# Four of nine taps of the interpolation matrices transposed by DMA, sampling two tiles behind

## The chip, the cores and the metric

The kernel runs on one core of one Trainium2 chip. The metric is the device time of one execution, in microseconds (us).

## What is computed

The input is x, four images of 128 channels and 64 x 64 pixels, in float32. Two layers follow each other.

```
# layer 0: attention over the 4096 pixels of each image
h = group_norm(x); q, k, v = split(qkv_w @ h + qkv_b)
x = x + proj_w @ (softmax(q^T k * C**-0.5) v) + proj_b

# layer 1: deformable convolution block
out = relu(batchnorm(conv2d(x, w1), g1, b1))
offsets = conv2d(out, w_off) + b_off          # 18 = 9 taps x (row, column)
out = batchnorm(deform_conv(out, offsets, w2), g2, b2)
return relu(out + x)

# deform_conv: for each pixel and each of 9 taps n
px = row + pn_x + off[..., :9];  py = col + pn_y + off[..., 9:]    # clipped
xo = bilinear interpolation of out at (px, py)
y  = sum over taps and channels of w2[:, :, tap] * xo[tap]
```

## The kernel before

All matrix products that need more than half precision are made of three products of f16 parts: `three` (L937 to L939) multiplies high by high, high by low and low by high, and adds them in PSUM.

The program has three parts: attention (until about 1710 us), the first convolution with the offset convolution (until about 2046 us), and the deformable stage, which the change touches. The deformable stage works on 128 tiles (q) of 128 pixels, 32 to an image; 16 tiles make a half image. A tile has 8 blocks (t) of 4 x 4 pixels. For each block the 120 pixels around it (a window of 10 rows by 12 columns) are in SBUF, one pixel to a partition, and for each of the 9 taps (k) an interpolation matrix of 128 pixels by 120 window positions tells how each output pixel is mixed from its window. These are the steps of a tile:

- SyncE loads the windows of two tiles at a time (`xt_windows`, L290 to L296): three transfers of 40 partitions and 8 KB each, into one of four buffers. The read pattern of a transfer has 10 rows as its outermost dimension, the written tile 40 partitions.
- GpSimd multiplies the row hats by the column hats into `interp` (SS, f32, 128 pixels x 9 taps x 120, two buffers), three instructions (L372). Before tile q it waits until TensorE has transposed tile q-2. Twice per half image it also computes the distances of the next one (L358, L363), which ScalarE turns into hats in four instructions at tiles 10 to 13 (L559, L562).
- TensorE transposes the nine matrices against an identity, three to a PSUM bank (L1105).
- ScalarE casts each bank to f16 (`interpT_hi`, L541), VectorE subtracts that from the bank to get the rest (`interpT_lo`, L876). Both tiles are laid out as block, tap, 16 pixels, in two buffers.
- TensorE samples: for each block a `three` with the window as weights and the 144 columns of the transposed matrices as moving operand (`sample`, L1117), 24 products in three sections. ScalarE and VectorE split the result into `sampled_hi` (L550) and `sampled_lo` (L884).
- TensorE applies the second convolution (`conv2`, L1126, 27 products of 128 columns), VectorE adds the result to `y_then_z` (L892) and takes statistics every fourth tile (L899).

The order on TensorE is written out by hand: in step g it does the transposes of tile q, then in three sections the sampling of tile q-1 and the convolution of tile q-2. The other engines follow the same steps. TensorE and VectorE run the steps in a loop over half images, ScalarE and GpSimd in one over pairs of half images, SyncE in one over images. Semaphores count each step; `after(eng, key, count)` waits for one. If all offsets are small, as with these inputs, the stage is passed through once.

In the attention part the kernel already transposes by DMA: SyncE issues transfers of 128 x 512 f16 (L242, L244), beside transposes on TensorE.

Of the kernel before, what the change touches and what calls it, by code (L numbers as in the profile page):

```python
# [17 lines left out]
F32 = mybir.dt.float32  # L18
# [19 lines left out]
TAPS = 9  # L38
# [21 lines left out]
NBUF = 4  # L60
SECT = ((0, 3), (3, 3), (6, 2))
# [26 lines left out]
def build(nc, x, weights, consts, out):  # L88
# [6 lines left out]
    with ctx:  # L95
# [3 lines left out]
        def sb_in(scope, name, shape, dt):  # L99
# [9 lines left out]
        ZT = sb_in(ctx, "zeros_f16", [128, 768], F16)  # L109
        CNT = sb_in(ctx, "pass_counts", [1, 6], I32)  # L110
        HIGH = sb_in(ctx, "offset_high", [128, GPI, NOFF], F32)
# [36 lines left out]
        XS = sb_in(l1, "xt_stage", [128, 2, 4, 2 * C], F16)  # L148
        l1a = ExitStack()
        XC = sb_in(l1a, "x1_rows", [128, 4, 512], F32)  # L150
# [11 lines left out]
        STh = sb_in(l1b, "interpT_hi", [128, 2, 8, TAPS, 16], F16)  # L162
        STl = sb_in(l1b, "interpT_lo", [128, 2, 8, TAPS, 16], F16)
# [26 lines left out]
        s_ld = [sem(f"windows_loaded{i}") for i in range(NBUF)]  # L190
        s_fx = [sem(f"final_loaded{i}") for i in range(B)]
# [12 lines left out]
            tt="interp_transposed", th="interpT_hi_ready", tl="interpT_lo_ready", mm="sampled",  # L204
# [18 lines left out]
        def _(sp):  # L223
# [36 lines left out]
            sp.wait_ge(s_pz, 1)  # L260
# [16 lines left out]
            for i in range(2):  # L277
                stored(sp, s_xs[i], B * NCH * 2)
            after(sp, "l1", L1_FLAG)
# [5 lines left out]
            with sp.Fori(0, ny) as iy:  # L285
                with sp.Fori(0, nx) as ix:
                    with sp.Fori(0, B) as b:
                        for i in range(HH // TW):

                            after(sp, "mm", (iy * SX + ix) * (3 * GROUPS) + b * (3 * GPI) + 6 * (i - (NBUF - 1)))  # L290
                            row = (iy + sy0) * WR + b * IMG_ROWS + (GUARD + TW * i - 3 - WR * (SY // 2))
                            slot = row * PITCH + (ix + sx0) * (WC // TW) + (0 - (WC // TW) * (SX // 2))
                            for a in range(WC // TW):
                                src = bass.AP(xt_dram.tensor, (slot + a) * (2 * C),
                                              [[PITCH * 2 * C, WR], [SLOTS * 2 * C, TW], [1, WW // TW * 2 * C]])
                                sp.dma_start(XW[WR * TW * a:WR * TW * a + WR * TW, i % NBUF, :, :], src).then_inc(s_ld[i % NBUF], 16)  # L296
# [11 lines left out]
        def _(po):  # L308
            for k in s:
                po.sem_inc(s[k], OPEN)  # L310
            for k in s_xo + s_xs + s_tr:
                po.sem_inc(k, OPEN)
# [921 lines left out]
```

## Time and profile before

| | us |
|---|---|
| median of 3 runs | 2662.31 |
| lowest and highest | 2656.64, 2663.07 |
| profiled execution | 2665.29 |
| its span, first to last instruction | 2663.5 |
| TensorE busy in the span | 2492.9 (94%) |
| VectorE busy | 1925.3 (72%) |
| ScalarE busy | 1823.4 (68%) |
| GpSimd busy | 953.9 (36%) |

The page gives each engine's busy time over the whole span, which mixes the three parts of the program. Its rows in 40 slices show them apart: a slice is 66.6 us, and the deformable stage fills the last nine but the very last. What one tile costs is read in stretches of 4 us inside a half image. Starts of instructions come from the timeline, where an idle time in square brackets stands with what ended it. Matmuls overlap in the pipeline, so the duration of one (220 ns and more) is longer than the distance between two starts.

### The profile page before, as it was taken

Reading aid. Unit: us, or ns where it says so; the run is one execution under the profiler, and the core shown is the slowest. Engines: PE = TensorE matmul, PEld = TensorE weight load, DVE = VectorE, ACT = ScalarE, POOL = GpSimd, SP = SyncE. Lnnn points to the kernel's source line nnn. Section 1 sums busy time; section 2 is a strip of 40 time slices with the busy share of each in tenths; the row PEclk is TensorE's granted clock in tenths of the full one; section 3 lists DMA queues with packets and bytes.
Section 4 is the critical chain, followed back from the end, with each engine's and each line's share of the span. In section 5 each row is a group of like instructions: output and inputs, shape, how many; then the busy total and the mean of one; then the engine's idle time right before and its main releaser. Section 6 shows DMA issues by size and latency. Waiting matters only on the chain.

```text
span 2663.5 us, 75563 instructions
## 1 busy us (share of the span) xinstructions
PE 2492.9 (94%) x27789; PEld 1960.8 (74%) x27789; DVE 1925.3 (72%) x3815; ACT 1823.4 (68%) x2963; POOL 953.9 (36%) x939
## 2 busy tenths in 40 slices
PE   4999999999999999999999999899975999999993
PEld 2777777777777777777777777644443999999993
DVE  6778877788877788887777777522264877877775
ACT  4778777777877777877777777511264766766664
POOL 1333333333333333333333333200012666656650
PEclk9999999999999999999999999899997999999997
DMA  2545554545564545554444444543122444333336
GB/s 78 123 92 96 94 114 91 95 95 94 96 116 86 96 96 92 95 90 84 94 96 95 95 94 95 143 136 132 37 73 79 138 117 121 116 110 116 111 106 253
DMA packets 642462, 278.30 MB, mean 104 GB/s; under 512 B 565665, under 2 KB 625569, under 8 KB 633889
## 3 DMA queue, kind: packets, MB, share of 16 engines
q1 hardware_dynamic: 642208, 274.82, 44.9%
q8 instruction: 171, 2.80, 0.5%
q14 instruction: 83, 0.67, 0.1%
HBM read 98.76 MB, written 41.68 MB: 53 GB/s over the span
## 4 chain that ended last, share of the span: by engine, by line
PE 89%; DVE 3%; DMA 2%; issue 2%; ACT 1%; SPq 1%; POOL 0%; DVEq 0%; POOLq 0%; ACTq 0%
PE psum L937 16%; PE psum L938 16%; PE psum L939 16%; PE psum L976 9%; PE psum L978 8%; PE psum L977 8%; PE psum L962 8%; PE psum L1105 5%; PE psum L1078 1%; DMA xt_scratch<-xt_stage 1%; DMA final<-x_scratch 1%; PE psum L1007 1%; SPq L276 0%; DVE padded_hi L842 0%; DMA probsT_dma_lo<-probs_lo 0%
## 5 line engine op out<-in xcount | busy, mean ns | idle before, releaser
L328 POOL TENSOR_TENSOR probs_lo<-probs,probs_hi 128x512 f16<-128x512 f32 x512 | 593.2, 1159 | 1085.7 <-ACT probs_hi L427 1085.7
L630 DVE TENSOR_REDUCE neg_max<-psum 128x1 f32<-128x1024 f32 x512 | 627.1, 1225 | 320.8 <-PE psum L939 320.4
L424 ACT ACTIVATE probs<-psum,exp_bias 128x1024 f32<-128x1024 f32 x512 | 570.8, 1115 | 193.3 <-DVE exp_bias L632 163.1
L937 PE MATMUL psum<-k_hi,q_hi 128*128 128x512 f16 x1024 | 389.3, 380 | 5.7 <-DVE vT_lo L744 4.0
L938 PE MATMUL psum<-k_lo,q_hi 128*128 128x512 f16 x1024 | 389.6, 380 | 0.0
L939 PE MATMUL psum<-k_hi,q_lo 128*128 128x512 f16 x1024 | 389.5, 380 | 0.0
L976 PE MATMUL psum<-vT_hi,probsT_dma_hi 128*128 128x129 f16 x2048 | 374.5, 221 | 4.3 <-DMA probsT_dma_lo<-probs_lo 4.3
L417 ACT ACTIVATE probsT_hi<-psum 128x512 f16<-128x512 f32 x512 | 303.7, 593 | 103.9 <-PE psum L962 103.9
L978 PE MATMUL psum<-vT_hi,probsT_lo 128*128 128x129 f16 x2048 | 374.3, 219 | 0.0
L976 PE MATMUL psum<-vT_hi,probsT_hi 128*128 128x129 f16 x2048 | 374.2, 221 | 0.0
L977 PE MATMUL psum<-vT_lo,probsT_hi 128*128 128x128 f16 x2048 | 374.1, 218 | 0.0
L978 PE MATMUL psum<-vT_hi,probsT_dma_lo 128*128 128x129 f16 x2048 | 374.1, 219 | 0.0
L977 PE MATMUL psum<-vT_lo,probsT_dma_hi 128*128 128x128 f16 x2048 | 374.0, 218 | 0.0
L372 POOL TENSOR_TENSOR interp<-row_hats,col_hats 128x360 f32<-128x360 f32 x384 | 294.7, 796 | 216.6 <-PE psum L1105 211.7
L640 DVE TENSOR_TENSOR probsT_lo<-psum,probsT_hi 128x512 f16<-128x512 f32 x512 | 350.1, 684 | 2.9 <-ACT probsT_hi L417 2.7
L427 ACT ACTIVATE probs_hi<-probs 128x512 f16<-128x512 f32 x512 | 322.6, 630 | 22.6 <-DMA probsT_dma_lo<-probs_lo 0.6
L962 PEld LDWEIGHTS psum<-constants,probs 128*128 128x128 f32 x2048 | 254.2, 141 | 94.3 <-issue 0.5
L962 PE MATMUL psum<-constants,probs 128*128 128x128 f32 x2048 | 307.9, 273 | 0.0
L876 DVE TENSOR_TENSOR interpT_lo<-psum,interpT_hi 120x384 f16<-120x384 f32 x384 | 191.5, 551 | 84.7 <-ACT interpT_hi L541 83.7
L550 ACT ACTIVATE sampled_hi<-psum 128x432 f16<-128x432 f32 (+1 forms) x384 | 182.6, 496 | 91.7 <-PE psum L939 91.7
L884 DVE TENSOR_TENSOR sampled_lo<-psum,sampled_hi 128x432 f16<-128x432 f32 (+1 forms) x384 | 207.0, 554 | 52.4 <-ACT sampled_hi L550 48.2
L541 ACT ACTIVATE interpT_hi<-psum 120x384 f16<-120x384 f32 x384 | 162.4, 491 | 87.5 <-PE psum L1105 85.2
(158 smaller groups left out, 5754.2 us busy)
## 6 DMA issues: line engine op xcount, KB each, us to landing
xt_windows<-xt_scratch SPq DMA_DIRECT2D x192, 320.0 KB
xt_scratch<-zeros_f SPq DMA_DIRECT2D x28, 576.0 KB, 4.0
x_image<-x SPq DMA_DIRECT2D x4, 2048.0 KB, 8.3
probsT_dma_hi<-probs_hi SPq DMA_TRANSPOSE x512, 2.4
probsT_dma_lo<-probs_lo SPq DMA_TRANSPOSE x512, 2.5
x_residual<-x SPq DMA_DIRECT2D x128, 64.0 KB, 2.1
x_scratch<-x_out SPq DMA_DIRECT2D x128, 64.0 KB, 1.8
x_rows<-x_scratch SPq DMA_DIRECT2D x32, 256.0 KB, 3.0
```

The lines of the kernel that those rows point to most:

```text
L328: po.tensor_tensor(PHl[:, j, :], P[:, j, 0:512], PHh[:, j, :], ALU.subtract).then_inc(s["pl"], 1)
L424: act.activation(P[:, j, :], sc, ACT.Exp, bias=NB[:, par, j:j + 1]).then_inc(s["exp"], 1)
L427: act.activation(PHh[:, j, :], P[:, j, 0:512], ACT.Copy).then_inc(s["ph"], 1)
L630: ve.tensor_reduce(NM[:, par, j:j + 1], sc, AX.X, ALU.max, negate=True).then_inc(s["mx"], 1)
L640: ve.tensor_tensor(PTl[:, k, :, :].rearrange("p m q -> p (m q)"), PS[:, 4 + j % 2, :], PTh[:, k, :, :].rearrange("p m q -> p (m q)"), ALU. ...
L937: pe.matmul(dst, lh, rh, start=start, stop=False)
L938: pe.matmul(dst, lh, rl, start=False, stop=False)
L939: return pe.matmul(dst, ll, rh, start=False, stop=stop)
L962: last = pe.transpose(PS[:, bank, 128 * m:128 * m + 128], P[:, j, 512 + 128 * m:512 + 128 * m + 128], ident)
L976: pe.matmul(dst, th, Vh[:, p, v, 0:129], start=m == 0, stop=False)
L977: pe.matmul(dst[:, 0:128], th, Vl[:, p, v, :], start=False, stop=False)
L978: last = pe.matmul(dst, tl, Vh[:, p, v, 0:129], start=False, stop=m == 7)
```

## The change

- Of the nine taps, 0 to 4 are still transposed by TensorE, in two banks of three and two (`PTAP`). Taps 5 to 8 (`DTAP` = 4) are split into f16 parts before the transpose: ScalarE casts them from `interp` to `interp_split` (SH, four buffers; `dma_taps_hi`), VectorE writes the rest beside them (`dma_taps_lo`).
- SyncE transposes both parts of the four taps in one transfer per tile, 128 x 1024 f16, from `interp_split` to the new tile `interpT` (ST). Before it, it waits for VectorE (`dl`) and until tile q-4 has been sampled. In its order stand the windows of two tiles, then two of these transfers.
- `interpT` replaces `interpT_hi` and `interpT_lo`. It has four buffers and is laid out as tap, part, pixel: TensorE's moving operand of a block is now nine runs of 16 elements, 256 elements apart.
- In step g TensorE does five transposes of tile q, the sampling of tile q-2 and the convolution of tile q-3. There is one more step at the end.
- GpSimd waits before tile q for the transposes and for VectorE's split of tile q-2.
- For room in SBUF, some small tiles (`zeros_f16`, `offset_high`, `xt_stage`) move to the tiles of the convolution part, and their clearing or computing moves behind the attention part.

```diff
+DTAP = 4
+PTAP = ((0, 3), (3, 2))
+T0 = TAPS - DTAP
...
-        XS = sb_in(l1, "xt_stage", [128, 2, 4, 2 * C], F16)
+        SH = sb_in(l1, "interp_split", [128, 4, DTAP, 2, 128], F16)
...
-        STh = sb_in(l1b, "interpT_hi", [128, 2, 8, TAPS, 16], F16)
-        STl = sb_in(l1b, "interpT_lo", [128, 2, 8, TAPS, 16], F16)
+        ST = sb_in(l1b, "interpT", [128, 4, TAPS, 2, 128], F16)
...
+                    def transposed(b, g):
+                        q = (iy * SX + ix) * GROUPS + b * GPI + g
+                        after(sp, "dl", q + 1)
+                        after(sp, "mm", q * 3 - 9)
+                        sp.sem_inc(s_go, 1)
+                        sp.dma_start_transpose(ST[:, g % 4, T0:TAPS, :, :].rearrange("p k e x -> p (k e) x"),
+                                               SH[:, g % 4, :, :, :].rearrange("p k e x -> p (k e x)")).then_inc(s_td[g % 4], 16)
+
+                    def image_steps(b, first):
                         for i in range(HH // TW):
...
+                            windows(b, i)
+                            if i or not first:
+                                transposed(b, 2 * i - 2)
+                                transposed(b, 2 * i - 1)
...
             def interp(q, hb, g):
-                after(po, "tt", q * 3 - 3)
+                after(po, "tt", q * 2 - 2)
+                after(po, "dl", q - 1)
...
+            def dma_taps_hi(q, g, hid):
+                after(act, "pr", q + 1)
+                stored(act, s_td[g % 4], hid * 4 + g // 4)
+                act.activation(SH[:, g % 4, :, 0, 0:KW], SS[:, g % 2, T0:TAPS, :], ACT.Copy).then_inc(s["dh"], 1)
+
             def interp_hi(q, g, i):
-                after(act, "tt", q * 3 + (i + 1))
+                k0, nk = PTAP[i]
+                after(act, "tt", q * 2 + (i + 1))
                 if i == 0:
-                    after(act, "mm", q * 3 - 3)
-                src = PS[0:KW, i, 0:384].rearrange("p (k t x) -> p k t x", k=3, t=8)
-                dst = STh[0:KW, g % 2, :, 3 * i:3 * i + 3, :].rearrange("p t k x -> p k t x")
-                act.activation(dst, src, ACT.Copy).then_inc(s["th"], 1)
+                    after(act, "mm", q * 3 - 9)
+                src = PS[0:KW, i, 0:128 * nk].rearrange("p (k x) -> p k x", k=nk)
+                act.activation(ST[0:KW, g % 4, k0:k0 + nk, 0, :], src, ACT.Copy).then_inc(s["th"], 1)
...
-                        for i in range(3):
+                        dma_taps_hi(q, g, hid)
+                        for i in range(2):
                             interp_hi(q, g, i)
                         if not last and g in (10, 11, 12, 13):
                             hats(hid + 1, 1 - hb, g - 10)
-                        if g or not first:
+                        if g >= 2 or not first:
                             for i in range(3):
-                                sampled(q - 1, (g + 1) % 2, i)
+                                sampled(q - 2, g % 2, i)
...
+            def dma_taps_lo(q, g):
+                after(ve, "dh", q + 1)
+                ve.tensor_tensor(SH[:, g % 4, :, 1, 0:KW], SS[:, g % 2, T0:TAPS, :], SH[:, g % 4, :, 0, 0:KW], ALU.subtract).then_inc(s["dl"], 1)
...
             def interp_transposes(q, g):
                 after(pe, "pr", q + 1)
-                for i in range(3):
-                    after(pe, "tl", q * 3 + (i - 2))
-                    for k in range(3):
-                        last = pe.transpose(PS[0:KW, i, 128 * k:128 * k + 128], SS[:, g % 2, 3 * i + k, :], ident)
+                for i, (k0, nk) in enumerate(PTAP):
+                    after(pe, "tl", q * 2 + (i - 1))
+                    for k in range(nk):
+                        last = pe.transpose(PS[0:KW, i, 128 * k:128 * k + 128], SS[:, g % 2, k0 + k, :], ident)
                     last.then_inc(s["tt"], 1)
...
-                    sh = STh[0:KW, g % 2, t, :, :].rearrange("p k x -> p (k x)")
-                    sl = STl[0:KW, g % 2, t, :, :].rearrange("p k x -> p (k x)")
-                    last = three(PS[:, 3 + i, 144 * (t - t0):144 * (t - t0) + 144], xw[:, 0:C], xw[:, C:2 * C], sh, sl, True, True)
+                    sh, sl = (ST[0:KW, g % 4, :, e, 16 * t:16 * t + 16] for e in range(2))
+                    dst = PS[:, 3 + i, 144 * (t - t0):144 * (t - t0) + 144].rearrange("p (k x) -> p k x", k=TAPS)
+                    last = three(dst, xw[:, 0:C], xw[:, C:2 * C], sh, sl, True, True)
...
                         for i in range(3):
-                            if g <= HALF and (g or not first):
-                                p = (g - 1) % HALF
+                            if g < HALF + 2 and (g >= 2 or not first):
+                                p = (g - 2) % HALF
...
+                                if i == 0:
+                                    pe.wait_ge(s_td[p % 4], (hid * 4 + ((g - 2) // 4 + 1)) * 16 + OPEN)
+                                sample(q - 2, p, i)
+                            if g >= 3 or not first:
+                                conv2(q - 3, (g + 1) % 2, i)
```

## Rows read from the trace of the kernel before

**Rows 1.** The page: the clock granted to TensorE, in 40 slices of the span.

```profile
PEclk9999999999999999999999999899997999999997
```

**Rows 2.** The chain of work in order of time: start, length in us, what.

```profile
2061.42 2.17 PE psum L1105 x9
...
2191.84 2.17 PE psum L1105 x9
...
2263.28 2.17 PE psum L1105 x9
...
2302.26 0.99 PE psum L1105 x9
2314.28 0.99 PE psum L1105 x9
```

**Rows 3.** The waits from 2050 to 2620 us: total, times, longest.

```profile
PE psum L1105 <- issue: 25.0, 6, 5.5
```

**Rows 4.** Stretches: length, busy PE, PEld, DVE, ACT, POOL, clock, DMA share, GB/s.

```profile
2278.00:2282.00 4.00, 4.00 (x64) 3.99 (x61) 3.26 (x8) 2.69 (x7) 2.71 (x4) 1.00 0.52 141
2282.00:2286.00 4.00, 4.00 (x64) 3.99 (x61) 3.77 (x9) 2.69 (x7) 4.00 (x4) 1.00 0.33 109
...
2314.00:2318.00 4.00, 4.00 (x64) 3.99 (x61) 3.94 (x9) 4.00 (x10) 2.30 (x3) 1.00 0.39 127
...
2610.00:2618.00 8.00, 7.43 (x118) 7.07 (x117) 6.14 (x14) 4.17 (x9) 0.00 (x0) 1.00 0.01 3
```

**Rows 5.** The same view, right behind a return of the loop.

```profile
2262.00:2264.00 2.00, 0.72 (x4) 0.73 (x5) 0.00 (x0) 0.00 (x0) 0.00 (x0) 0.54 0.06 12
...
2268.00:2270.00 2.00, 2.00 (x29) 2.00 (x28) 0.61 (x1) 0.79 (x2) 0.00 (x0) 0.75 0.00 0
```

**Rows 6.** Timeline inside a half image: start, us, engine, line, operation, idle before.

```profile
2270.66 1.25 ACT L541 ACTIVATE interpT_hi<-psum 120x384 f16<-120x384 f32 x3 [0.50 <-PE psum L1105]
...
2271.18 1.49 DVE L876 TENSOR_TENSOR interpT_lo<-psum,interpT_hi 120x384 f16<-120x384 f32 x3 [0.53 <-ACT interpT_hi L541]
...
2275.29 0.80 POOL L372 TENSOR_TENSOR interp<-row_hats,col_hats 128x360 f32<-128x360 f32 x1 [1.70 <-PE psum L1105]
...
2301.93 0.22 PE L937 MATMUL psum<-sampled_hi,weights_hi 128*128 128x128 f16 x1
...
2302.05 0.22 PE L939 MATMUL psum<-sampled_hi,weights_lo 128*128 128x128 f16 x1
```

**Rows 7.** DMA from 2302.5 to 2309.5, 40 slices of 0.175 us.

```profile
DMA  0092405639990488155655664979462922000000
...
DMA packets 151, 1.00 MB, mean 143 GB/s; under 512 B 30, under 2 KB 30, under 8 KB 30
...
q1 hardware_dynamic: 150, 0.98, 49.6%
```

**Rows 8.** Timeline of SyncE's queue: start and duration of an issue.

```profile
999.26 1.19 SPq L242 DMA_TRANSPOSE probsT_dma_hi<-probs_hi  x1
...
2302.04 0.29 SPq L296 DMA_DIRECT2D xt_windows<-xt_scratch  x1
```

**Rows 9.** Groups by line and form, 2030 to 2600: count, busy us, mean ns.

```profile
L876 DVE TENSOR_TENSOR interpT_lo<-psum,interpT_hi 120x384 f16<-120x384 f32 x375 | 187.0, 551 | 83.1 <-ACT interpT_hi L541 82.1
L541 ACT ACTIVATE interpT_hi<-psum 120x384 f16<-120x384 f32 x375 | 158.7, 491 | 86.0 <-PE psum L1105 83.6
...
L884 DVE TENSOR_TENSOR sampled_lo<-psum,sampled_hi 128x432 f16<-128x432 f32 x246 | 145.2, 603 | 35.8 <-ACT sampled_hi L550 31.9
L550 ACT ACTIVATE sampled_hi<-psum 128x432 f16<-128x432 f32 x247 | 128.4, 535 | 53.1 <-PE psum L939 53.1
...
L550 ACT ACTIVATE sampled_hi<-psum 128x288 f16<-128x288 f32 x123 | 51.4, 418 | 33.7 <-PE psum L939 33.7
```

**Rows 10.** Stretch holding one transposing transfer of the attention part; columns as above.

```profile
1000.40:1001.30 0.90, 0.90 (x12) 0.60 (x10) 0.90 (x4) 0.74 (x1) 0.07 (x1) 1.00 0.75 146
```

**Rows 11.** DMA issues by line, 200 to 1800 us: median us from issue to landing.

```profile
probsT_dma_hi<-probs_hi SPq DMA_TRANSPOSE x467, 2.4
```

More of the change, by code:

```diff
@@ L190, in build @@
         s_ld = [sem(f"windows_loaded{i}") for i in range(NBUF)]
+        s_td = [sem(f"interp_dma_transposed{i}") for i in range(4)]
+        s_go = sem("interp_transpose_released")
         s_fx = [sem(f"final_loaded{i}") for i in range(B)]
@@ L286, in _, with windows @@
                 with sp.Fori(0, nx) as ix:
-                    with sp.Fori(0, B) as b:
-                        for i in range(HH // TW):
[L290 to L296, printed above, removed]
+                    def windows(b, i):
+                        after(sp, "mm", (iy * SX + ix) * (3 * GROUPS) + b * (3 * GPI) + 6 * (i - (NBUF - 1)))
+                        row = (iy + sy0) * WR + b * IMG_ROWS + (GUARD + TW * i - 3 - WR * (SY // 2))
+                        slot = row * PITCH + (ix + sx0) * (WC // TW) + (0 - (WC // TW) * (SX // 2))
+                        for a in range(WC // TW):
+                            src = bass.AP(xt_dram.tensor, (slot + a) * (2 * C),
+                                          [[PITCH * 2 * C, WR], [SLOTS * 2 * C, TW], [1, WW // TW * 2 * C]])
+                            sp.dma_start(XW[WR * TW * a:WR * TW * a + WR * TW, i % NBUF, :, :], src).then_inc(s_ld[i % NBUF], 16)
@@ L297, in _ @@
+                    image_steps(0, True)
+                    with sp.Fori(1, B) as b:
+                        image_steps(b, False)
+                    transposed(B - 1, GPI - 2)
+                    transposed(B - 1, GPI - 1)
             for i in range(4 * B):
@@ L584, in _ @@
                 half_image(NHALF - 1, 1, False, True)
-                for i in range(3):
-                    sampled(n * GROUPS + (GROUPS - 1), 1, i)
+                for g in range(2):
+                    for i in range(3):
+                        sampled(n * GROUPS + (GROUPS - 2 + g), g, i)
             after(act, "l1", L1_AB2)
@@ L904, in half_image @@
                         if g < HALF:
-                            for i in range(3):
-                                interp_lo(q0 + g, g, i)
-                        if 3 <= g < HALF + 3:
-                            z_add(q0 + (g - 3), h, g - 3)
-                        elif g < 3 and not first:
-                            z_add(q0 + (g - 3), h - 1, g - 3 + HALF)
-                        if g <= HALF and (g or not first):
-                            for i in range(3):
-                                sampled_lo(q0 + (g - 1), (g + 1) % 2, i)
+                            dma_taps_lo(q0 + g, g)
+                            for i in range(2):
+                                interp_lo(q0 + g, g, i)
+                        if 4 <= g < HALF + 4:
+                            z_add(q0 + (g - 4), h, g - 4)
+                        elif g < 4 and not first:
+                            z_add(q0 + (g - 4), h - 1, g - 4 + HALF)
+                        if g < HALF + 2 and (g >= 2 or not first):
+                            for i in range(3):
+                                sampled_lo(q0 + (g - 2), g % 2, i)
                         if g >= 4 and g % 4 == 3:
@@ L1110, in sample @@
                 if i == 0:
-                    after(pe, "tl", q * 3 + 3)
+                    after(pe, "tl", q * 2 + 2)
                 after(pe, "xl", q * 3 + (i - 2))
@@ L1149, in _ @@
                     half_image(h, range(HALF), False)
-                half_image(NHALF - 1, range(HALF, HALF + 2), False)
+                half_image(NHALF - 1, range(HALF, HALF + 3), False)
 def schedule(eng, unit, extra):
```

39 lines of the change are left out of this document (19 added, 20 removed).

## The prediction

> **What bounds the kernel now.** I read the page's clock slices first: in the second part the clock dips at regular distances [rows 1]. The changed stage is the last one before the output. It begins with the first transpose of an interpolation matrix at 2061.4 [rows 2] and ends near 2617 (7.43 of the 8 us from 2610 on are busy [rows 4]). It handles 128 tiles of 128 pixels in 8 half images of 16.
>
> The stretches inside a half image [rows 4] decide what limits it. TensorE is busy 4.00 of 4.00 us, VectorE 3.26 (3.77 where the statistics fall in), ScalarE 2.69 (4.00 where it makes hats), GpSimd 2.7 to 4.0. In the chain the transposes of tiles three apart start at 2302.26 and 2314.28 [rows 2]. So a tile costs 4.01 us, and TensorE's instruction stream sets it; that ScalarE at 4.00 does not hold TensorE up says that the buffers absorb about a tile's lag. Six times TensorE waits for "issue" before the transposes, 25.0 us in all [rows 3]: the returns of the half-image loop, in which all engines stand still, and after which the granted clock is 0.5 for some 6 us (0.54 at the restart, 0.75 six us on [rows 5]; nine transposes then take 2.17 us [rows 2]). Two such starts lie 2263.28 - 2191.84 = 71.4 us apart [rows 2], where 16 tiles take 64.1; a jump costs 7.3 us with its slow clock. Check: 8 x 64.1 + 6 x 7.3 = 556.6, and the stage is 2617 - 2061.4 = 555.6.
>
> The last resource is the DMA. One load of windows (three transfers, for two tiles) moves 0.98 MB, in slices 2 to 33, from 2302.85 to 2308.4, and the 49.6% of the 7 us is 3.5 us of all 16 engines, so 0.63 of the 5.5 us [rows 7]; it ends in 30 small packets, ten to a transfer. Together: a window transfer runs on ten engines. Over the 8 us of two tiles the share is (0.52 + 0.33) / 2 = 0.43 [rows 4], or 0.43 x 8 x 16 / 10 = 5.5 us of each of the ten. They are idle for 2.5.
>
> **The change part by part.**
> *TensorE, removed.* Nine transposes hold the chain for 0.99 us [rows 2], 0.11 each. Four go: 0.44 us per tile, x 128 = 56 us. All of it lies on the path. The pace of TensorE alone becomes 4.01 - 0.44 = 3.57 us.
> *TensorE, altered.* The sampling products (24 per tile, 144 columns) now read their moving operand as nine runs of 16 halves, 512 B apart. No row of TensorE has such runs. Below, nothing can be gained (the operand was contiguous). Above: reading 4-byte elements of the identity, a 128-column product takes 0.11 against 0.057 for 128 two-byte columns (two of them from 2301.93 to 2302.05) [rows 6], so a doubling, 24 x 0.06 = 1.4 us per tile. The nearest rows are VectorE's and ScalarE's writes to `sampled_lo` and `sampled_hi` in runs of 16 halves, at 603 and 535 ns for 432 elements, against 551 and 491 for 384: 1.1 and 0.9 ns per extra element, full rate [rows 9]. I take 0.
> *ScalarE.* Three casts of 384 (1.25 us back to back [rows 6]) become one of 480 from SBUF, one of 384 and one of 256. From 0.83 ns per element and 0.17 to 0.2 fixed (491 for 384, 418 for 288 [rows 9]): 0.60 + 0.49 + 0.38, back to back 1.3 us. Even. A hat instruction adds at least 4.00 - 2.69 = 1.3 us to a tile [rows 4], I take 1.4. Such tiles have 2.69 - 1.25 + 1.3 + 1.4 = 4.1 us of ScalarE against 3.57: four tiles, 2.1 us of lag, of which a tile's slack takes about half. 1 us per half image, only where nothing else binds.
> *VectorE.* Three subtractions of 384 (551 each) become 480, 384, 256: with 1.04 ns per element, 0.65 + 0.55 + 0.42, 1.5 us back to back as now [rows 6, 9]. VectorE's 3.26 us, and 0.13 as a mean for statistics, stay below 3.57, but only just (95%).
> *GpSimd.* It gets a wait on VectorE's new subtraction (`dl`) before it overwrites `interp`. Queued behind the wait are only the next interpolation and at two tiles in 16 the distances. It now waits 1.7 us per tile for TensorE [rows 6]; ScalarE is free 0.50 us before 2270.66 [rows 6], about when that step's transposes start (2302.26 - 8 x 4.01 = 2270.2 [rows 2]); the cast of 480 and the subtraction follow, so `dl` comes 0.60 + 0.65 = 1.3 us into step q. The 3 x 0.80 us of work that it releases are for tile q+2 and done at 3.7. No cost. The moved clears of small buffers (0.7 us and less) stand at stage borders; I count nothing for them.
> *SyncE's queue.* A transfer of 512 columns is issued in 1.19 us and lands after 2.4 [rows 8, 11]; 1024 columns I take as twice the issue, 2.4 us (bounds 1.2 and 2.4), landing at 3.6. Per two tiles: 2 x 2.4 + 3 x 0.29 for the window issues [rows 8] = 5.7 us of 7.1, and some register work. The queue holds. Behind each transposing transfer's wait for `dl` are the next windows; they are wanted five steps later, no cost.
> *The ten engines.* A 512-column transposing transfer occupies all 16 engines: 0.9 us at a share of 0.75 [rows 10], so 0.68 us of every engine; 1024 columns 1.36. Bounds: 1.2 (a tenth less, should two packets overlap more) and 2.4 (if the engines are held for as long as it is issued). Per two tiles a window engine must do the load and two transfers. The load: 5.5 us by the stretch and by the share; its first third of a microsecond is start-up, which a queue that never empties hides; I take 5.2. Sum 5.2 + 2 x 1.36 = **7.9 us** for two tiles, against 2 x 3.57 = 7.14 on TensorE. So the ten window engines are late next, and the saved transposes are mostly handed back.
> The Trainium skill (DMA: Bandwidth & Descriptors, section "Why a DMA increments its semaphore by 16 and not by 1") states that a hardware-generated transfer uses the largest count up to 16 that divides both outer dimensions, the lowest-numbered ones. The outer dimensions here are 10 rows and 40 partitions, so ten; the trace agrees (ten endings per transfer). Had the loads spread over all 16, the same work would be 0.43 x 8 + 2.7 = 6.2 us, and the change would be hidden below TensorE.
>
> **How far this reaches.** A sample needs its transfer two steps later: from `dl` (1.3 us into step q) to 0.55 into step q+2, 7.14 - 0.75 = 6.4 us. Behind a window load the even tile's transfer must wait: the load's data begin about 3.3 us after the odd tile's transfer was issued (2.4 + 0.8 and a little: issue at 2302.04, first data 2302.85 [rows 7, 8]), run 5.2, then 1.36 and 0.35 to land: 10.2 - 3.57 = 6.6 us. Just missed. So after a jump, where the queue has run empty and the first tiles are slow, two pairs go at 7.14; then the shortfall shows: 0.2, and 5 x 0.75 us for the other pairs. A half image behind a jump: 7.3 + 16 x 3.57 + 4.0 = 68.4 instead of 71.4, a gain of 3.0, times 6 = 18. The first two half images run without a jump: 16 pairs at 7.9 and not 8.01, and a first pair or two free: 3 us. The first sample waits for the first transfer behind two window loads: 2 us lost. Sum: 18 + 3 - 2 = 19 us. Against the profiled execution (2665.3, span 2663.5) this gives 2646; it was 3.0 above the median, so **2643**.
>
> **The rivals.**
> *Hidden transfers.* If loads and transposes pass each other better than the sum has it (7.1 us or less for two tiles), TensorE stays the bound: 56 - 8 (ScalarE's lag) - 2 = 46, time 2662 - 46 = 2616. For it: shares of 0.7 to 0.9 occur in slices of the load [rows 7], so ten engines are not all there is to it. Against: the means. 0.18.
> *Nothing left.* The same mechanism with the sum at 8.1 to 8.6 us: gains at the jumps only, eaten by the fill: 2654 to 2670, taken as 2661. 0.18.
> *Slower: a transfer that holds the window engines longer.* Nothing in the trace has transposes and window loads side by side. From 1.75 us per transfer the ten engines need 8.7 us per pair, more than now. At 2.0 (halfway between 1.36 and the issue time, with the load at 5.3) a pair is 9.3: 16 x 1.3 = 21 us in the first two halves; behind jumps 7.3 + 2 x 7.1 + 6 x 9.3 - 1 = 76.3, 5 us more, x 6 = 29: 2712. 0.15.
> *Slower: VectorE and GpSimd lock each other.* The new subtraction is the first per-tile VectorE instruction of this stage with both inputs in SBUF. If it had to wait for a running `interp` product (0.80 us [rows 6]), VectorE would need 3.4 + 0.8 = 4.2 us per tile, 0.2 over now: 128 x 0.2 = 26, 2688. Against it: by the order above GpSimd has finished at 3.7, 0.5 us before the next subtraction starts (3.57 + 0.65), and waits for it afterwards; only the two tiles with distances can collide. 0.05.
> The Trainium skill (SBUF — State Buffer, section "Who interferes with whom") states this rule: a VectorE instruction with two SBUF inputs and a GpSimd instruction that reads SBUF exclude each other for a whole instruction. No row of this trace shows the two side by side.
> *Slower: runs of 16 halves.* At the upper bound, 3.57 + 1.4 = 5.0 us per tile, 128 us: 2790. 0.04.
>
> **How the numbers follow.** The forecast has 0.40 (own range 2628 to 2654), the others 0.18, 0.18, 0.15, 0.05, 0.04. The measurement can tell 0.3% from nothing, 8 us: faster is below 2654, slower above 2670. Faster 0.40 + 0.18 = 0.58; same 0.18; slower 0.24. The range 2608 to 2700 takes in hidden transfers and the two nearer slower cases up to 1.9 us per transfer.
>
> **What the new profile would show.** L1105's successor at five per tile, 0.55 us in the chain. Starts of the tiles' transposes unevenly spaced: about 3.6 us between the two tiles of a pair after a jump, later one wait per pair on `interpT` from the DMA, before the sampling of an even tile. The DMA share 0.75 to 0.8 over a pair; at 3.6 us throughout with no DMA wait, hidden transfers hold. A wait of `interp_split` on GpSimd, or `interp` products above 0.8 us, would show the lock; sampling products spaced above 0.062 us the runs. I am wrong if a 1024-column transfer keeps an engine for much other than 1.4 us, or if the window loads' 5.2 us shrink or stretch beside it.

## The result

The kernel got slower: 2737.5 us median (2735.8 to 2745.5), against 2661.2 for the kernel before in the same series, a ratio of 1.0295 [1.0271, 1.0320]. The forecast was 2643, and the time lies outside its range (2608 to 2700). The profiled execution took 2737.3 us, with a span of 2734.6.

The page of the kernel after: busy time, TensorE's slices, the clock, the DMA share.

```profile
PE 2461.6 (90%) x27277; PEld 1917.1 (70%) x27277; DVE 1942.0 (71%) x3815; ACT 1823.3 (67%) x2963; POOL 955.0 (35%) x940
...
PE   5999999999999999999999999899766878786873
...
PEclk9999999999999999999999999999888999999996
DMA  2645555544554445544544444532229999999998
```

In the changed stage (slices 30 to 38 and the start of 39, counted from 0) the DMA row stands at 9 in every whole slice. The DMA share is the sum of the times of all packets over the time of 16 engines; packets overlap, so it can exceed 1. TensorE, at 9 in slices 31 to 38 before, falls to 6 to 8 there. The stage as one stretch, first before, then after (columns as in [rows 4]):

```profile
2061.00:2617.00 556.00, 530.49 (x7653) 526.93 (x7653) 431.80 (x925) 378.93 (x796) 332.30 (x396) 0.96 0.39 113
```

```profile
2062.00:2691.00 629.00, 499.86 (x7168) 483.06 (x7168) 450.70 (x930) 379.27 (x796) 333.42 (x395) 0.93 0.98 153
```

The stage grew by 73 us, and the span by 2734.6 - 2663.5 = 71, so the whole loss is here. TensorE's busy time shrank by 31 us (at a mean clock of 0.93, before 0.96), its idle time rose from 26 to 129, and the DMA share went from 0.39 to 0.98. The waits of the stage (total, times, longest), to be set beside [rows 3]:

```profile
POOL interp L399 <- DVE interp_split L907: 217.6, 116, 6.6
...
PEld psum L976 <- issue: 71.7, 35, 4.4
...
PE psum L976 <- DMA interpT<-interp_split: 53.1, 29, 4.2
PE psum L1144 <- issue: 48.9, 7, 10.3
...
PE psum L976 <- DVE interpT L913: 19.2, 10, 2.8
```

Three things are new. The first: before the sampling products (L976) TensorE waits for the transfer, 29 times by the name of the DMA. Ten more waits there are put down to VectorE's work on a later tile, which the sampling does not wait for; in six of them the last packets of a transposing transfer end 0.06 to 0.08 us before TensorE goes on, so these are counted with the others. Together they are 39 waits in 64 pairs of tiles, 72 us, 1.9 us each. The PEld line, "issue" 71.7 us, is no further time: the weight load stands in the same waits, as at 2637.74.

```profile
2637.74 0.10 PEld L976 LDWEIGHTS psum<-interpT,xt_windows 120*128 120x128 f16 x1 [1.87 <-issue]
```

The second: the waits before the transposes, 25.0 us in [rows 3], are 48.9. Six of the seven are the loop's returns (10.3, 5.2, 6.0, 5.2, 10.2 and 9.6 us, 46.5 together); the seventh, 2.5 us at 2376.7, stands one tile behind a return.

The third: the granted clock falls to half inside half images too, where it did so before only at the returns. There are ten such stretches of 3.4 us, each beside a wait for a transfer (of 1.9 to 4.2 us). Here are two (columns as in [rows 4]):

```profile
2112.80:2116.20 3.40, 3.40 (x32) 3.40 (x31) 0.61 (x1) 0.79 (x2) 1.33 (x2) 0.50 1.51 203
...
2252.80:2256.20 3.40, 3.40 (x33) 3.40 (x31) 1.68 (x4) 1.43 (x3) 0.07 (x1) 0.50 1.32 205
```

In all TensorE is at half clock for 92 us of the stage, before 44. The first line of the list of waits, 217.6 us, is idle time of GpSimd, which follows TensorE and costs nothing by itself.

The starts of the transposes after the last return (timeline of TensorE: start, us, what, idle before) show the pace:

```profile
2609.32 1.32 PE L1144 MATMUL psum<-constants,interp 128*120 128x128 f32 x5 [9.56 <-issue]
...
2615.42 0.71 PE L1144 MATMUL psum<-constants,interp 128*120 128x128 f32 x5
...
2618.99 0.71 PE L1144 MATMUL psum<-constants,interp 128*120 128x128 f32 x5
...
2622.56 0.71 PE L1144 MATMUL psum<-constants,interp 128*120 128x128 f32 x5
...
2626.13 0.71 PE L1144 MATMUL psum<-constants,interp 128*120 128x128 f32 x5
...
2631.84 0.71 PE L1144 MATMUL psum<-constants,interp 128*120 128x128 f32 x5
...
2635.41 0.71 PE L1144 MATMUL psum<-constants,interp 128*120 128x128 f32 x5
2637.75 0.23 PE L976 MATMUL psum<-interpT,xt_windows 120*128 120x144 f16 x1 [1.63 <-DMA interpT<-interp_split]
2640.78 0.71 PE L1144 MATMUL psum<-constants,interp 128*120 128x128 f32 x5
```

Three steps of 3.57 us, then 5.71, 3.57, 5.37: where nothing is waited for, TensorE keeps exactly the pace of the forecast, and in each pair one tile waits for its transfer. A pair takes 8.9 to 9.4 us (2631.84 to 2640.78, next start of the kind 2650.16), not 7.9.

### The profile page after: what moved, and what is told of

Read it like the earlier page. It is cut to its first block, busy times and chain, and to the rows that moved or that the text cites. A ratio compares the mean times of both kernels' runs of the same rounds, so it can differ in the third digit from the quotient of the medians.

```text
span 2734.6 us, 76234 instructions
## 1 busy us (share of the span) xinstructions
PE 2461.6 (90%) x27277; PEld 1917.1 (70%) x27277; DVE 1942.0 (71%) x3815; ACT 1823.3 (67%) x2963; POOL 955.0 (35%) x940
## 4 chain that ended last, share of the span: by engine, by line
PE 78%; DMA 8%; DVE 5%; issue 5%; ACT 2%; SPq 1%; POOL 0%; DVEq 0%; ACTq 0%; POOLq 0%
PE psum L976 14%; PE psum L978 14%; PE psum L977 14%; PE psum L1015 8%; PE psum L1017 8%; PE psum L1016 8%; PE psum L1001 8%; DMA interpT<-interp_split 6%; PE psum L1117 1%; PE psum L1144 1%; DVE interp_split L907 1%; DMA final<-x_scratch 1%; PE psum L1046 1%; ACT interp_split L565 1%; DVE padded_hi L876 0%
## 5 line engine op out<-in xcount | busy, mean ns | idle before, releaser
L976 PE MATMUL psum<-k_hi,q_hi 128*128 128x512 f16 x1024 | 388.9, 380 | 6.5 <-DVE vT_lo L777 4.0
L399 POOL TENSOR_TENSOR interp<-row_hats,col_hats 128x360 f32<-128x360 f32 x384 | 295.7, 798 | 283.1 <-DVE interp_split L907 217.6
L976 PE MATMUL psum<-interpT,xt_windows 120*128 120x144 f16 x1024 | 218.6, 235 | 73.4 <-DMA interpT<-interp_split 53.1
L976 PE MATMUL psum<-sampled_hi,weights_hi 128*128 128x128 f16 x1152 | 223.2, 226 | 1.2 <-DVE sampled_lo L922 0.6
```

The source lines that it names most:

```text
L976: pe.matmul(dst, lh, rh, start=start, stop=False)
```

## The experiments

Theory A: the DMA engines pace the stage, as in the forecast, with a pair at 9.2 instead of 7.9. Rival B: the lock of VectorE and GpSimd. Rival C: the runs of 16 halves. Two more came up later: D, that the place of a transfer behind a whole load costs more than its work, and F, that code which the sequencers fetch through the same DMA engines holds up the transfers.

**Without the transfers (e1).** The transfer is dropped, with TensorE's wait for it; the four taps' columns of `ST` hold zeros.

```diff
-                        sp.dma_start_transpose(ST[:, g % 4, T0:TAPS, :, :].rearrange("p k e x -> p (k e) x"),
-                                               SH[:, g % 4, :, :, :].rearrange("p k e x -> p (k e x)")).then_inc(s_td[g % 4], 16)
...
+            po.memset(ST[:, :, T0:TAPS, :, :], 0.0).then_inc(s_pz, 1)
...
-                stored(act, s_td[g % 4], hid * 4 + g // 4)
+                after(act, "mm", q * 3 - 9)
```

> The changed kernel without its 128 transposing transfers (the four taps' columns of `interpT` stay zero, so this part of the sampling is left out of the result); casts, subtractions, waits and order of all engines stay. Theory A (the ten window engines carry the loss: 5.7 us of load plus two transfers of 1.75 us are 9.2 us for two tiles): every wait of the sampling on the transfers and the long loop returns (10 us) go, tiles start 3.57 us apart, time 2620 to 2640. Theory B (the lock of VectorE and GpSimd carries it: `interp_split` subtractions of 2 to 3 us beside the distances): those stay, time above 2700. Theory C (runs of 16 halves slow the sampling): above 2700 too, with sampling products more than 0.062 us apart.

Measured: 2639.9, ratio 0.9926 [0.9903, 0.9949]. All the transfers together cost 2737.5 - 2639.9 = 98 us. That is at the upper end of what theory A expected, and far from B and C, which would have left it above 2700. But it is not the time of an unhindered TensorE either; that is taken up at f1.

**Loads over 16 engines (e2).** Each window transfer is cut into 32 and 8 partitions.

```diff
-                                          [[PITCH * 2 * C, WR], [SLOTS * 2 * C, TW], [1, WW // TW * 2 * C]])
...
+                            for r0, nr in ((0, 32), (32, 8)):
...
+                                              [[SLOTS * 2 * C, nr], [1, WW // TW * 2 * C]])
```

> The changed kernel with each window transfer split into one of 32 and one of 8 partitions, so that the larger runs on 16 engines. The busiest engines then have 9 packets of 8 KB per load and not 12. Theory A: per two tiles 9 x 0.46 + 2 x 1.6 = 7.3 us, close to TensorE's 7.14; the shares of the waits for the transfers fall to a few us, the time to 2640 to 2665 (with the lock still in). A rival (the loads are limited by the memory, whatever engines they use): within 10 us of 2737.

Measured: 2792.7, ratio 1.0512 [1.0479, 1.0545]. The remedy that the forecast's sum called for makes it worse by another 2 points. The same 400 us of e2 and of the kernel after (columns as above):

```profile
2200.00:2600.00 400.00, 304.55 (x4122) 295.80 (x4121) 258.03 (x528) 218.37 (x456) 196.38 (x229) 0.87 1.12 140
```

```profile
2200.00:2600.00 400.00, 315.32 (x4541) 305.92 (x4538) 284.73 (x589) 243.02 (x508) 215.03 (x253) 0.93 0.99 155
```

Fewer bytes per second (140 against 155 GB/s) follow from the longer time alone; what tells is the higher share with them. The packets take longer for the same bytes: one of 8 KB has a median of 0.62 us in e2 and 0.39 in the kernel after, and a whole load 6.5 where it was 5.6. From issue to landing a transposing transfer takes 7.5 us in e2 and 5.4 in the kernel after (DMA issues, 2200 to 2600, first e2, then after):

```profile
interpT<-interp_split SPq DMA_TRANSPOSE x73, 7.5
```

```profile
interpT<-interp_split SPq DMA_TRANSPOSE x81, 5.4
```

So more engines did not make the load faster; the forecast's sentence that loads over 16 engines would hide the change is wrong. Why is open: the edit also makes six transfers out of three, and no run separates the two.

**Short distances (e3), and both edits (e4).** GpSimd's `row_hats`/`col_hats` distances (L389), 3.1 us each, are cut into four instructions of four tiles. e4 has this and the edit of e2.

```diff
+                for m in range(4):
+                    last = po.tensor_tensor(dst[:, hb, 4 * m:4 * m + 4, :, :],
...
+                last.then_inc(s["hd"], 1)
```

> The changed kernel with each of GpSimd's two distance instructions of a half image cut into four. If VectorE's subtraction waits for a running GpSimd instruction, its longest time falls from 3.1 us to about 1.5, and its mean from 814 to below 720 ns. Theory A alone: the lock delays an odd tile's transfer, which the busy engines make up for in part; time 2737 minus 5 to 15. Theory B: 2737 minus 30 or more.

> Both edits: window loads on 16 engines and the distances in quarters. Theory A with the lock as a second cost: 2620 to 2645, below the kernel before by more than 15 us. If only one of the two mattered, it is within 5 us of that one's run.

Measured: e3 2740.7, 1.0305 [1.0282, 1.0327]; e4 2794.6, 1.0499 [1.0475, 1.0522], both as without the short distances. Theory A had expected a gain of 5 to 15 us in e3 and B one of 30 or more, and e4 was to come to 2645 or less; none of this came. Yet the lock is there. Timeline of the kernel after, VectorE and GpSimd:

```profile
2163.11 3.06 DVE L907 TENSOR_TENSOR interp_split<-interp,interp_split 128x480 f16<-128x480 f32 x1
```

```profile
2162.53 3.12 POOL L389 TENSOR_TENSOR col_hats<-constants,offsets 128x1728 f32<-128x1728 f32 x1
```

A subtraction that takes 0.66 us otherwise takes 3.06 and ends half a microsecond behind the GpSimd instruction beside it. By the groups (mean ns after the comma), first after, then e3:

```profile
L907 DVE TENSOR_TENSOR interp_split<-interp,interp_split 128x480 f16<-128x480 f32 x128 | 104.2, 814 | 27.1 <-ACT interp_split L565 24.4
```

```profile
L905 DVE TENSOR_TENSOR interp_split<-interp,interp_split 128x480 f16<-128x480 f32 x128 | 90.2, 705 | 28.0 <-ACT interp_split L563 25.2
```

The edit takes 14 us out of these subtractions and none out of the time (the longest subtraction falls from 3.06 to 1.37 us, so the lock did get shorter): behind a transfer that comes late, the lock costs nothing.

**Without transfers and with short distances (f1).**

> The run without transfers (the four taps' columns of `interpT` stay zero, so this part of the sampling is left out), with GpSimd's distances in quarters too. It prices the lock where nothing else binds. If the waits of VectorE's subtraction for the distances (14 of 2 to 3 us in the changed kernel) lie on the path once the transfers are gone: 2640 minus 10 to 25, so 2615 to 2630, with the subtraction's mean near 700 ns. If another cost holds that run 24 us above 2616: unchanged at 2640.

Measured: 2622.7, 0.9858 [0.9842, 0.9874]. Against e1 the lock is worth 17 us, once nothing else is late. f1 is also what the forecast called hidden transfers (2616), so TensorE's side of the sum holds to 7 us. The Trainium skill (SBUF — State Buffer, section "Who interferes with whom") has a VectorE instruction with two SBUF inputs and a GpSimd instruction that reads SBUF shut each other out. The trace agrees, with the 3.06 us above.

**Half the bytes in the loads (f2).** The transfers stay, only half of each window is fetched; the second tile of each pair samples the first one's.

```diff
-                                          [[PITCH * 2 * C, WR], [SLOTS * 2 * C, TW], [1, WW // TW * 2 * C]])
+                                          [[PITCH * 2 * C, WR], [SLOTS * 2 * C, TW], [1, WW // TW * C]])
```

> The changed kernel with window loads of half the bytes: each transfer brings 8 of the 16 blocks' windows, and both tiles of a pair are sampled from these (so every second tile samples wrong windows). All transposing transfers stay. Theory A (load and transfers add up on the DMA engines): 2.8 + 2 x 1.75 = 6.3 us for two tiles, under TensorE's 7.14: 2630 to 2655, as without transfers. If the transposing transfers cost the time by themselves, above 2700.

Measured: 2634.4, 0.9896 [0.9879, 0.9912]: with all the transfers, 103 us less than the kernel after, and no more than without transfers (e1; the intervals overlap). This is what theory A expected. So the transfers with half the load beside them do no harm; it is full loads and transfers on the same engines.

**Another order (f3), and f3 with short distances (g1).** The three window transfers of a load are issued one by one, with the tiles' transfers between them.

```diff
-                            windows(b, i)
+                            windows(b, i, (0,))
                             if i or not first:
                                 transposed(b, 2 * i - 2)
+                            windows(b, i, (1,))
+                            if i or not first:
                                 transposed(b, 2 * i - 1)
+                            windows(b, i, (2,))
```

> The changed kernel with another order on SyncE's queue: the three window transfers of a load are issued one by one, before, between and behind the two transposing transfers of a pair, so that none waits behind a whole load. Work and bytes are the same. Theory A (the sum of the work of the engines decides): 2737 plus or minus 10. Theory D (what decides is that a transposing transfer stands behind a whole load, and that its second half waits for the slowest engine): 2710 or less.

> The changed kernel with the window transfers issued one by one between the transposing ones, and the distances in quarters. In the changed kernel's own order the quarters gave nothing (2741 against 2738). If the lock counts as soon as the transfers bind less: 2703 minus 10 to 17, 2686 to 2693. If the transfers still cover it: 2700 or more.

Measured: f3 2703.1, 1.0147 [1.0114, 1.0180]; g1 2701.4, 1.0154 [1.0128, 1.0179]. The order alone is worth 34 us, the same bytes and transfers given. Theory A by itself, a sum of the engines' work, expected 2737 plus or minus 10 here; D, 2710 or less. So the sum is not all. The waits of f3:

```profile
PE psum L979 <- DMA interpT<-interp_split: 46.4, 30, 3.9
PE psum L1147 <- issue: 43.6, 7, 9.7
```

Both kinds of wait remain (one of the seven "issue" waits, 1.2 us, is again no return). The lock again costs nothing where the DMA is late.

**A finer order (g3).** Each tile's transfer is cut into two of 512 columns, and the window transfers stand between the four.

```diff
+                            for j in range(7):
+                                if j % 2:
+                                    windows(b, i, (j // 2,))
+                                elif i or not first:
+                                    transposed(b, 2 * i - 2 + j // 4, j % 4)
```

> Four taps by DMA, each tile's transfer cut into two of 512 columns, and between each two of them one of the three window transfers; distances in quarters. No transfer stands behind more than one window transfer (1.3 us). Window transfers that run alone take 4.0 us together instead of 5.6. Theory D: 4.0 + 2 x 1.5 = 7.0 us for two tiles, below TensorE's 7.14: 2630 to 2665, and the loop returns near 4 us again. If the sum of the engines' work decides whatever the order: 2690 to 2740.

Measured: 2736.3, 1.0290 [1.0262, 1.0318]. The expectation fell. Finer turns gain nothing over the first order, so "the shorter the turn, the less is lost" is wrong; seven turns may cost what they save, but that is only an argument.

**Fewer taps by DMA (f4, g2, g4).** `DTAP` is 2 or 3 instead of 4; TensorE transposes seven or six. f4 has the order of the kernel after, g2 and g4 that of g1 and its short distances.

```diff
-DTAP = 4
-PTAP = ((0, 3), (3, 2))
+DTAP = 2
+PTAP = ((0, 4), (4, 3))
```

> The changed kernel with two taps by DMA and not four: transfers of 512 columns, seven transposes on TensorE. Theory A: the engines need 5.7 + 2 x 0.9 = 7.5 us for two tiles, TensorE 2 x (4.01 - 0.22) = 7.58: balanced, 28 us less than the kernel before, less about 10 for lock and fill: 2640 to 2655. If transfers cost a fixed part (waiting behind the load, two passes), 2660 to 2700.

> As the run before, with two taps by DMA and seven transposes on TensorE. Theory D (a transfer's place behind the loads costs more than its work): the 18 us that two taps lost against the kernel before vanish, 2645 to 2660. If the work of the engines decided, order changes nothing: 2675 to 2680.

> As the first of these, with three taps by DMA (768 columns) and six transposes on TensorE, which needs 3.68 us per tile. Between its neighbours with four and two taps if the engines' work decides in each: 2665 to 2690.

Measured: f4 2679.4, 1.0075 [1.0058, 1.0092]; g4 2682.7, 1.0084 [1.0054, 1.0114]; g2 2656.8, 0.9988 [0.9976, 1.0001]. With the order and distances of g1, four, three and two taps give 2701, 2683 and 2657: each tap less on the DMA saves 19 and 26 us, although TensorE has 0.11 x 128 = 14 us more to do for it [rows 2]. For f4 theory A had 2640 to 2655, and a fixed part of the price 2660 to 2700, as measured; for g2, D had 2645 to 2660, as measured, and A 2675 or more. g2 is the best of these that computes everything, and no faster than the kernel before. Its waits:

```profile
PE psum L977 <- DMA interpT<-interp_split: 5.9, 8, 1.2
...
PE psum L1145 <- issue: 26.5, 6, 7.1
```

**Idle transfers beside the kernel before (h1, h2).** The kernel before keeps its nine transposes and issues, for each tile, one transposing transfer of 128 x 1024 (h1) or 128 x 512 (h2) whose output nobody reads.

```diff
+                                after(sp, "pr", q - 1)
...
+                                sp.dma_start_transpose(DU[:, g % 2, :, :], WH[:, 0:1024]).then_inc(s_du[g % 2], 16)
```

> The kernel before, unchanged in its computing, with one idle transposing transfer of 128 x 1024 f16 per tile added to SyncE's queue (from the weights into a tile that nobody reads). No engine waits for them; only the window loads share their queue and engines. Theory A (work of the DMA engines: 5.7 + 2 x 1.75 = 9.2 us for two tiles against TensorE's 8.02): the loads come late, 56 x 1.2 = 67 us more, and the loop returns grow by some 20: 2720 to 2750. Theory D (only the place of a needed transfer behind a load costs): below 2690. If a transfer took 1.36 us of the engines as predicted, 8.4 us for two tiles, 2675 to 2700.

> The same with idle transfers of 512 columns. Theory A: 5.7 + 2 x 0.9 = 7.5 us for two tiles, below TensorE's 8.02: 2660 to 2675. If a transfer has a fixed price (the engines that are done wait for the slowest), it is more than half of the run with 1024 columns: 2690 or more.

Measured: h1 2682.5, 1.0074 [1.0056, 1.0092]; h2 2674.6, 1.0048 [1.0030, 1.0066]. Inside a half image h1 loses nothing: TensorE is busy 8.00 of 8.00 us while the DMA share is 1.07.

```profile
2108.00:2116.00 8.00, 8.00 (x124) 7.98 (x122) 6.92 (x16) 7.40 (x15) 4.59 (x7) 1.00 1.07 195
```

Theory A with its pair of 9.2 had expected 2720 or more; why so little is lost is taken up below. The loss is at the returns, 43.1 against 25.0 in [rows 3]: 18 of the 20 to 22 us.

```profile
PE psum L1114 <- issue: 43.1, 6, 9.5
```

So filling the DMA engines, with nobody waiting for the data, lengthens a return of the loop by 3 us. Where the share stays low the returns stay as before: 24.5 us in e1 and f1, 25.8 in f2, 26.5 in g2. Here is f2:

```profile
PE psum L1144 <- issue: 25.8, 6, 5.9
```

**More code (i1, i2).** If code fetches through the DMA engines set the pace, more code should cost much in the kernel after and little in the one before. 48 increments of an unused semaphore stand ahead of each tile on GpSimd, in i1 (after) and i2 (before).

```diff
+                for _ in range(48):
+                    po.sem_inc(s_no, 1)
```

> The changed kernel with 48 counting instructions more per tile on GpSimd, on a semaphore that nobody waits for, ahead of its waits; GpSimd idles longer than they take. They only add code: 6 KB per two tiles, so some 24 fetches of 16 KB more over the stage. Theory F (a code fetch holds one DMA engine for a microsecond, and while transposing transfers run all 16 wait for that engine: 1.4 us per fetch): 2738 plus 15 to 35. If fetches are not a cause of the 9.2 us: 2738 plus 0 to 5.

> The same counting instructions in the kernel before, which has no transposing transfers in this stage: the control. Both theories: 2661 plus 0 to 8 (the loop returns may grow a little).

Measured: i1 2753.2, 1.0349 [1.0331, 1.0366], 16 us over the kernel after; i2 2670.4, 1.0037 [1.0026, 1.0048], 10 over before. F had expected 15 to 35 us in i1 and 0 to 8 in i2. The net effect, some 5 us, decides nothing. The added fetches came as small packets on another queue (after, then i1, 2080 to 2660):

```profile
q8 instruction: 70, 1.15, 0.8%
q14 instruction: 28, 0.23, 0.1%
```

```profile
q8 instruction: 70, 1.15, 0.8%
q14 instruction: 77, 0.63, 0.3%
```

The 16 KB packets of q8, which are the suspects, stayed at 70: the edit did not move what it was to move.

## What a pair of tiles consists of

A load takes 5.6 to 5.8 us in full traffic. Between its end and the next load's start lie two transposing transfers: about 2 us in some pairs, 3.5 in most. The packets of the kernel after show 61 such spaces between full loads. In 56 a code packet of q8 is in flight, and these take 3.1 us or more, 3.6 in the median; the five without one take 1.8 to 2.2. Here is a long one, 2643.4 to 2647.0, in slices of 0.09 us:

```profile
GB/s 102 119 125 148 128 128 128 46 0 0 228 293 282 299 268 439 273 267 279 267 91 0 0 0 0 0 9 9 9 9 9 9 11 9 11 193 282 293 290 290
...
q8 instruction: 1, 0.02, 1.7%
```

And one without, from h1, 2371.8 to 2374.0, in slices of 0.055 us, with no q8 row:

```profile
GB/s 84 107 126 116 135 158 126 130 144 135 116 112 33 0 0 0 5 261 298 293 289 293 289 284 252 271 279 298 284 298 293 293 289 289 284 298 279 293 289 298
```

In this stretch of h1 the traffic at about 290 GB/s runs on to the end. In the one of the kernel after it stops for 1.3 us: 0 GB/s for five slices, then 9 to 11 for nine, then 290 again. The packets' records do not name their engine. But at 9 GB/s the packets come one behind the other, 28 in all, and the stop lies about 512 packets from either end of its transfer. So the reading is that a transfer goes in rounds of 512 small packets, 32 to each of 16 engines, and that the next round starts when the slowest engine is done; one engine that fetches code for a microsecond would make sixteen stand. The fetches are not new. From 2200 to 2600 the kernel before has 56 of them, and the kernel after 51 (before, then after):

```profile
q8 instruction: 56, 0.92, 1.0%
```

```profile
q8 instruction: 51, 0.84, 0.9%
```

What is new is where they fall. From 2064 to 2610 the kernel before has 75; 67 of them overlap packets of a window load and 8 fall into idle time, and TensorE, which is busy without a gap inside a half image [rows 4], waits for none of them there. In the same stretch of the kernel after 44 of 67 fall into transposing transfers alone.

h1 makes the same comparison inside one program. Of its 62 spaces, 31 have a code packet in flight, with a median of 3.5 us, and 31 have none, with a median of 2.0. Only 16 of its 73 fetches from 2064 to 2610 fall into transposing transfers alone, the others mostly into loads. So its pairs are a mixture of long and short ones, and no engine waits for its transfers; this fits that TensorE keeps its pace inside a half image. Why the fetches meet the transfers so much more often in the kernel after is not known. All this is read from traces; no edit took the fetches out (i1 could not), so that they cause the pair's excess is likely and not shown.

## Why the prediction was wrong

- **TensorE's step** (4.01 - 0.44 = 3.57): right to the last digit, in every unblocked step above. But the sum let TensorE's clock fall only at the returns. Its busy time shrank by 31 us and not by 56, with a mean clock of 0.93 where it was 0.96.
- **Runs of 16 halves**: no cost. f1 at 2622.7 leaves no room for one, and the sampling products start 0.06 us apart (2637.75, .82, .88, .94) for 144 columns.
- **ScalarE's and VectorE's sums**: no visible error; neither engine ends a wait of weight beyond the transfers, and f1 is 7 us above the sum.
- **The window engines' sum, 5.2 + 2 x 1.36 = 7.9**: the mechanism is right (e1, f2), and so are the free pairs after a jump (2615.42 to 2626.13 at 3.57) and the one wait per pair (seen in 39 of 64). But f3 shows that a sum of work is not all: the same work in another order takes 34 us less. Both terms were too small: 5.6 to 5.8 for the load, 3.5 in place of 2.7 for two transfers, 9.2 together. The price of a transfer was a share of 0.75 over 0.9 us, read where little else was in the queue [rows 10]; that counts how long engines are occupied, not how long they stand for each other. Where nothing disturbs it the forecast's price was, if anything, too high (2.2 against 2.72, pair 7.8). Why two transfers take 3.5 us is the open part, with the code fetches as the likely cause. Two pairs go free behind the start of the stage and behind each of six returns, so about 50 of 64 are blocked; 50 x 1.3 = 65 us is the estimate.
- **The returns, 7.3 us each, "unchanged"**: they were costed without a thought for the DMA. They are 46.5 against 25.0, 21 us. h1 shows nearly the same growth (18 us) with no change of the program but the traffic. 65 + 21 = 86, of the 91 us between the forecast for the profiled execution (2646) and 2737.3.
- **The same 91 us on TensorE**: the forecast's 19 us of gain are 56 us less work and so 37 us of waiting for transfers. Measured were 31 us less busy time (25 short), 72 us of waiting for transfers (35 over), 24 more before the transposes, and 7 more of smaller waits: 25 + 35 + 24 + 7 = 91. The 65 us of the pairs appear here as the 35 us and most of the 25: a tile that runs at half clock while the transfers set the pace waits less.
- **The landing**: the sum had the even tile land 6.6 us after the step that makes it begins, 0.2 too late. From issue to landing the median over all tiles is 5.4 us and the longest 12.1; TensorE's 39 waits average 1.9 us, where the sum had 0.2 and then 0.75 us per pair. The issue of 1024 columns was bounded by 1.2 and 2.4 and taken as 2.4; it takes 1.25, as in the row of `transposed` (min/median/max ns, first and last start):

```profile
L307 SPq DMA_TRANSPOSE interpT<-interp_split x124: 1231/1252/3283, 2079.3 to 2678.6; - x124
...
DMA to landing us min/median/max: 3.1/5.4/12.1
```

  The queue's own time was thus never a limit.
- **Ten engines**: the reading was right, the conclusion drawn from it (16 would hide the change) wrong, by e2 (with the reserve stated there).
- **The rivals.** The one on the slower side, a transfer that holds the engines longer, came true nearly in its numbers: 9.3 us per pair, 2712 us. It had 0.15, because the price of a transfer was taken from a quiet stretch. With 21 us for the returns it gives 2733. Part of that is luck: its 2.0 us per transfer were said to lie halfway to an issue time of 2.4 us (halfway is 1.88), and the issue takes 1.25; measured are 5.6 for the load and 1.8 per transfer. The lock was put at 0.80 us on two tiles in 16; where it met the distances it was 2 to 3 us. It costs 17 us where the transfers are away, and nothing here.

## What to carry to other kernels

A transposing transfer priced in a quiet stretch can be priced too low: near a DMA share of 1, measure what the transfers take there, here 0.8 us more than priced for two transfers of 128 x 1024. The program's code comes through the DMA queues as well (q8 and q14), so look where its packets fall; if a loop's return is slow already, fill the DMA engines and it gets slower (25 to 43 us for six returns with idle transfers). Where the forecast leaves an engine waiting, ask what the waits do to its clock. Before cutting a load finer to spread it over more engines, measure what one costs when many run: here the spread cost 2 points more.

## What was not expected of the hardware

- The same 120 x 8 KB load on 16 instead of ten engines took longer (medians of 6.5 and 5.6 us), and its packets of 8 KB 0.62 us instead of 0.39.
- With a code packet of 16 KB inside a transposing transfer, the traffic falls from 290 GB/s to 0 and then 9, for 1.3 us in the stretch above. Of the long stops between loads in the kernel after (44), each has a code packet in flight.
- A transposing transfer is issued in 1.19 us with 512 columns [rows 8] and 1.25 with 1024: twice the columns hardly lengthen the issue.
- Still open: why three turns (f3) gain 34 us and seven (g3) none, and how the growth of a return comes about, whether by the code or by the data that the loop's head waits for; and why the fetches meet the transfers in 56 of 61 spaces. The DMA share alone doesn't set that growth: g3 is as full as the kernel after, and its returns sum to 31.2 us.
